# Sums placed beside values, act ends summed on TensorE, two more places for y, and later scaling in a two-act attention kernel

## The reference, cut to what matters

```
x = x + squared(layernorm(x))   # linear-attention layer: scores squared, causal, divided by their sum
x = x + gated(layernorm(x))     # softmax attention, keys and values picked per token by a top-1 gate
x = x + mqa(layernorm(x))       # softmax attention, one key and value head for all query heads
x = x + gated(layernorm(x))
# squared: q, k normalised over the head's 32 channels after gamma and beta
attn = where(causal, einsum(q, k) ** 2, 0);  o = einsum(attn, v) / (sum(attn) + EPS);  o @ Wo.T
# gated, mqa
att = softmax(where(causal, q k / sqrt(32), -inf));  y = einsum(att, v)   # mqa: then y @ out_w.T + out_b
```

## Time and profile before

| | |
|---|---|
| median of 3 runs | 3931.25 us |
| profiled execution | 3928.55 us |
| its span, first to last instruction | 3926.8 us |
| mean granted TensorE clock | 0.982 |
| PE busy | 3609.9 us (92%) |
| POOL busy | 2977.9 us (76%) |
| DVE busy | 2146.6 us (55%) |
| ACT busy | 1621.9 us (41%) |

### The profile page before, as it was taken

How to read it: one execution, slowest core, us unless ns; L and a number is a source line. 1 busy time by engine, 2 the same in 40 slices (tenths; PEclk the granted TensorE clock), 3 DMA queues, 4 the chain that set the end, 5 groups by cost and what they waited for, 6 DMA issues and landing times.

```text
span 3926.8 us, 66685 instructions
## 1 busy us (share of the span) xinstructions
PE 3609.9 (92%) x25570; PEld 1449.9 (37%) x25570; DVE 2146.6 (55%) x5132; ACT 1621.9 (41%) x2433; POOL 2977.9 (76%) x2207
## 2 busy tenths in 40 slices
PE   7999999997999999999888898998999999999976
PEld 5443434332333333333333333333333333333322
DVE  1222322233466766667666666565666666676663
ACT  3554545555033333434444434343333334343333
POOL 4988788897067777778888888887768677686786
PEclk9999999999999999999999999999999999999987
DMA  2001101011110110200101010100101001010010
GB/s 75 28 6 33 33 22 44 9 63 38 49 33 1 31 36 1 65 1 24 43 17 49 7 49 12 36 31 20 47 1 41 25 9 57 1 55 1 7 39 33
DMA packets 63286, 115.02 MB, mean 29 GB/s; under 512 B 8576, under 2 KB 9088, under 8 KB 62976
## 3 DMA queue, kind: packets, MB, share of 16 engines
q1 hardware_dynamic: 62976, 110.75, 8.7%
HBM read 77.17 MB, written 33.55 MB: 28 GB/s over the span
## 4 chain that ended last, share of the span: by engine, by line
PE 60%; ACT 5%; DVE 4%; POOL 3%; issue 2%; DMA 0%; POOLq 0%; ACTq 0%; DVEq 0%
PE banks L1144 12%; PE banks L1191 11%; PE banks L1238 10%; PE banks L1176 9%; PE banks L1137 8%; ACT probs_soft L880 4%; PE banks L1173 4%; PE banks L1337 2%; POOL added_soft L791 2%; DVE banks L976 1%; DVE maxima_soft L971 1%; PE banks L1205 1%; PE banks L1321 1%; POOL added_soft L784 0%; PE banks L1150 0%
## 5 line engine op out<-in xcount | busy, mean ns | idle before, releaser
L880 ACT ACTIVATE probs_soft<-banks 128x1024 f32<-128x1024 f32 (+1 forms) x960 | 848.5, 936 | 1147.8 <-PE banks L1176 1110.2
L791 POOL TENSOR_TENSOR added_soft<-added_soft,probs_soft 128x512 f32<-128x512 f32 (+1 forms) x380 | 1153.4, 3035 | 20.9 <-POOL added_soft L784 5.9
L976 DVE CUSTOM_DVE_ANT_0 banks<-banks,mask 128x128 f32<-128x128 f32 (+3 forms) x1536 | 701.1, 526 | 456.5 <-PE banks L1191 456.2
L971 DVE TENSOR_REDUCE maxima_soft<-banks 128x2 f32<-128x1024 f32 x384 | 452.4, 1221 | 358.7 <-PE banks L1191 358.5
L1191 PE MATMUL banks<-k_soft,q_soft 32*128 32x512 f32 (+3 forms) x4608 | 500.3, 526 | 73.3 <-ACT probs_soft L880 71.7
L1137 PE MATMUL banks<-xnT,wide 128*128 128x512 f32 x1024 | 506.8, 618 | 6.0 <-ACT shift_soft L863 1.9
L886 ACT ACTIVATE probs_squared<-banks,key_scale_squared 128x512 f32<-128x512 f32 (+3 forms) x768 | 379.2, 590 | 316.4 <-PE banks L1176 306.4
L1144 PE MATMUL banks<-wide,xnT 128*128 128x512 f32 x1024 | 498.7, 614 | 0.2 <-ACT shift_soft L863 0.2
L1176 PE MATMUL banks<-q_soft,k_soft 32*128 32x512 f32 (+3 forms) x4608 | 475.1, 495 | 0.0
L784 POOL TENSOR_TENSOR added_soft<-probs_soft 128x2048 f32<-128x2048 f32 x48 | 216.6, 4513 | 329.0 <-ACT probs_soft L880 323.2
L1238 PE MATMUL banks<-probs_soft,v_soft 128*32 128x512 f32 (+3 forms) x4608 | 419.9, 498 | 10.7 <-POOL probs_soft L768 3.8
(11 more groups left out here) (136 smaller groups left out, 4026.2 us busy)
## 6 DMA issues: line engine op xcount, KB each, us to landing
tiles<-out SPq DMA_DIRECT2D x96, 256.0 KB, 2.7
rest_soft<-out SPq DMA_DIRECT2D x96, 256.0 KB, 3.0
out<-rest_soft SPq DMA_DIRECT2D x96, 256.0 KB, 2.1
tiles<-in_x SPq DMA_DIRECT2D x32, 256.0 KB, 2.8
rest_squared<-in_x SPq DMA_DIRECT2D x32, 256.0 KB, 2.8
out<-rest_squared SPq DMA_DIRECT2D x32, 256.0 KB, 2.0
wide<-in_gated_wqkvT SPq DMA_DIRECT2D x3, 1024.0 KB, 7.5
probs_squared<-in_squared_wk SPq DMA_DIRECT2D x1, 1024.0 KB, 5.6
```

What stands on the lines that cost most here:

```text
L791: ins = pool.tensor_tensor(sums, sums, slot(ph, n)[:, :, col:col + width], ALU.add)
L880: ins = act.activation(slot(ph, n)[:, 2 * a:2 * a + 2, 0:width], score_pair(e, a)[:, :, 0:width], ACT.Exp, scale=SCALE)
L971: ins = dve.reduce_max(m["maxima"][:, ph % 2, 2 * a:2 * a + 2, t, p], score_pair(e, a)[:, :, col:col + width], AX_X)
L976: ins = dve.tensor_tensor_reduce(scores, scores, k["mask"][:, CHUNK - width:CHUNK], 1.0, MASKED, ALU.add, ALU.max, m["maxima"][:, ph % 2, ...
```

## The change

`SUMS_AT` puts the sums one half earlier, into the halves that hold values (9 and 15). `LAST_PART` hands bursts 5 and 6 of an act's last phase from POOL's adds to TensorE; the last sum comes ahead of av C and in two steps, all but the last two bursts in the first. The scaling becomes an event behind the first statistics. `y` gets 8 places in act 2. "merged" gets the deadline `2 * HALVES + 4`, and in the last stage of act 2 `3 * HALVES + 4` (it was `2 * HALVES + 6`).

```
-Y_RING = 6
+Y_RING = {False: 6, True: 8}
...
-LAST_PART = (7, 8, 9)
+LAST_PART = (5, 6, 7, 8, 9)
+
+LAST_TWO = (8, 9)
...
-SUMS_AT = (16, 10)
+SUMS_AT = (15, 9)
...
-        events = head[0] + [("raw_weights",), ("own_weights",)] + head[1]
+        events = head[0] + [("raw_weights",), ("own_weights",)] + head[1] + [("scaled",)]
...
-        work += [(parted(merged), 2 * HALVES + 6), (parted(later + first), (3 if kinds[s + 1:s + 2] != ["squared"] else NG) * HALVES - 2),
+        work += [(parted(merged), (3 if soft and s == stages - 1 else 2) * HALVES + 4), (parted(later + first), (3 if kinds[s + 1:s + 2] != ["squared"] else NG) * HALVES - 2),
...
-    events += [("av", last, "C"), ("sm", last, 1), ("last_nrm", last)]
+    events += [("more", ("sm", last, 1)), ("sm", last, 1), ("av", last, "C"), ("last_nrm", last)]
...
-                elif u == "raw_weights":
+                elif u == "scaled":
                     dve.wait_ge(sg.raw_in, DMA * RAW_WEIGHTS)
                     dve.tensor_scalar(m["scaled"][:], k["centre"][:], m["gamma"][:, 0:1], None, ALU.mult).then_inc(sg.scaled, 1)
...
                 elif u == "sm":
                     _, ph, c = e
                     out = free(e)
...
                     final = ph == NG * len(stages) - 1 and c == NC - 1
...
+                    def add_up(cells, q0, width, start, stop):
+
+                        for i in range(HG):
+                            ins = pe.matmul(out[D * i:D * i + D, q0:q0 + width], k["ones"][:], cells[:, i, :], start=start, stop=stop,
+                                            skip_group_check=not soft)
+                        return ins
+
+                    if e not in begun:
+                        if not soft:
+                            pe.wait_ge(sg.query_squares, place["qsq", ph, c] + 1)
+                            pe.matmul(out, k["head_eps"][:].rearrange("p i d -> p (i d)"), m["query_square"][:, c], start=True, stop=True)
+                        pe.wait_ge(sg.probs_added, len(ADDS) * ph + CHUNK_ADDS[c] - (len(LAST_PART) if final else 0))
+                        ins = add_up(m["added"][:, c], 0, CHUNK, soft, not final)
+                        begun[e] = 1
                     if final:
...
+                        for n in LAST_PART[:-len(LAST_TWO)] if opening else LAST_TWO:
+                            pe.wait_ge(sg.probs_ready, 2 * (of_kind["keys", ph, n] + 1))
+                            if KEY_BURSTS[n][1] != "B":
+                                pe.wait_ge(sg.probs_masked, masks_until(ph, None, n))
+                            for kb, q0, width, col in KEY_BURSTS[n][2]:
+                                ins = add_up(slot(ph, n)[:, :, col:col + width], q0, width, False, n == LAST_PART[-1] or not soft)
                     ready(e, ins)
```

More of the change, by code:

```diff
@@ L544, in act_buffers @@
         "q": sb("q", [P, NG, T]),
-        "y": sb("y", [P, Y_RING, T]),
+        "y": sb("y", [P, Y_RING[soft], T]),
         "sums": sb("sums", [P, NC, CHUNK]),
@@ L633, in y_of @@
     def y_of(ph):
-        return m["y"][:, ph % Y_RING, :]
+        return m["y"][:, ph % Y_RING[soft], :]
     def v_of(ph):
@@ L653, in masks_until @@
         masked = [o for o, burst in enumerate(KEY_BURSTS) if burst[1] != "B"]
-        last = n if n is not None else parts_of(part)[0][-1]
+        last = parts_of(part)[0][-1] if n is None else n
         return len(masked) * ph + sum(o <= last for o in masked)
@@ L922, in _ @@
                     c = "AB".index(part)
-                    if ph >= Y_RING and part == "A":
-                        wait_work(act, ("out", (ph - Y_RING) // NG, NT - 1))
+                    if ph >= Y_RING[soft] and part == "A":
+                        wait_work(act, ("out", (ph - Y_RING[soft]) // NG, NT - 1))
                     take_out(e, y_of(ph)[:, CHUNK * c:CHUNK * c + CHUNK], work[:, bank(e), :])
@@ L1198, in _ @@
                     out = free(e)
-                    if not soft:
-                        pe.wait_ge(sg.query_squares, place["qsq", ph, c] + 1)
-                        pe.matmul(out, k["head_eps"][:].rearrange("p i d -> p (i d)"), m["query_square"][:, c], start=True, stop=True)
                     final = ph == NG * len(stages) - 1 and c == NC - 1
[L1203 to L1206, removed]
@@ L1207, in _ @@
-                    if final:
[L1208 to L1213, removed]
+                    def add_up(cells, q0, width, start, stop):
[3 more added lines that the diff above has]
+                        return ins
```

## The result

The kernel after takes 4051.64 us (median of 4 runs, 4044.87 to 4059.35) against 3928.59 of the kernel before (4 runs beside it). The ratio is 1.0309, 95% interval 1.0276 to 1.0341: 3.1% slower, where 0.3% was forecast and the range ended at 3968. Its profiled execution has a span of 4057.6 us and a granted clock of 0.965.

A forecast was written before the change was run, and what follows sets the result against it. TensorE was taken to bound the middle of act 2, POOL's adds the very end. On 3928.55 us: -7.7 - 2.4 - 9 - 1.5 + 34 = +13.4, so 3942 us; 8-in-10 range 3897 to 3968.

The forecast's parts named there:

- Sums beside values: 128 sums moved directly behind av A or av B, in both acts: +34 us, bounds -27 and +100.
- The length of a wait: A sum behind values waits 0.78 us until ACT empties the bank; 0.65 net of the 0.13 saved.
- count: Sums that find a unit open when values end, and so wait for the bank: 81 of 128.
- The cover: Halves without values lose two covers per phase: 8 bare steps at 1.0 us each, +8.
- The relief: Pieces close waits where sums stood alone in about 48 halves, -14; DVE's row maxima get through sooner, -7.
- The sign that was to confirm the forecast: In TensorE's waits, a new row of sums waiting for ACT's copy of y, some 60 times at 0.7 to 0.8.
- The third rival: Where pieces are scarce, above all mqa stages, 35 halves stand bare instead of 8: 3975 us; chance 0.12.
- Its own sign: The wait of L1191 (rows bursts) for ACT grows beyond 80 us.
- Last but one results: Four transposing units leave phase 45 for 46 and 47, where they hide: gain 1.5 us, bounds -4 to +3 in time.
- Later scaling: At the start, scaling behind the statistics lets the fold start at 15.1 instead of 22.89: gain 7.7 us.
- the end of act 2: Without POOL's adds, 7.6 of TensorE's 7.90 us wait go, and the first reciprocal comes sooner: gain 9, bounds 3 and 11.
- The end of act 1: Chunk 0's product comes 1.6 us sooner and the first reciprocal 0.8: gain 2.4, bounds 0 and 4.

The follow-up runs named there:

- The doubled copy: Kernel after, but ACT copies the values of A and B to y twice and only the second copy frees the bank: 4079.87 us, ratio 1.0375.
- units were closed: Planner ends every open unit before av A and av B: on the kernel after 4085.82 us; with SUMS_AT = (16, 10) there, 3983.86 us.
- the sums alone: Kernel before with SUMS_AT = (15, 9) and nothing else of the change: 4033.51 us, ratio 1.026.
- the filled version with the sums back: Kernel after with SUMS_AT = (16, 10), act 1's old deadline, and four unused matmuls in each of 40 bare steps: 3894.89 us, ratio 0.991.
- sums back: Kernel after with SUMS_AT = (16, 10), so all of the change but the sums beside values: 3931.5 us, ratio 0.9998.
- the same version without fillers: Kernel after with SUMS_AT = (16, 10) and act 1's merged deadline back at 2 * HALVES + 6: 3912.92 us, ratio 0.9957.
- the version with both deadlines back: Kernel after, sums beside values, with merged's deadline back at 2 * HALVES + 6 in both acts: 4033.92 us, ratio 1.0261.

## Why the prediction was wrong

**Sums beside values** is the step that failed: forecast +34, measured alone +102, just above its upper bound of +100. Inside it:

- *The length of a wait* was right, 0.75 measured for 0.78. Its *count* was not: 59 for 81. "Units of four pieces stay open about as often" was the error. With the sum in their half, the values' halves take other pieces, and the order of the kernel after has an open unit at the end of av A in 23 phases of act 2 (38 before). What a wait costs in all stays between two estimates: 0.6 to 0.8 of its length by the doubled copy, 26 to 34 us for the 44 us of them; or 0.9 each, 54 us, if the 59 bare steps that took their place when units were closed cost 1.5 each as the other 34 did.
- *The cover* was mis-sized: "I take 8 of them" bare steps, and there are 32 more (29 in act 2; the sums alone add 31). A stage that is short of pieces gets five (the last gated stage ahead of mqa and the first three mqa stages), the last stage of all six. 1.0 us each was about right for idle time. What was missing was the slow matmuls behind it: 1.5 a step where only bare steps were added. At that price 31 steps are 47 us where 8 stood in the sum, and 55 of the 102 are left for the waits and all else; an estimate, which the split by stages above bears out in its order of size.
- *The relief* (-7 for DVE, -14 for closed waits) never came: those waits grew, to 70.6 and 27.5 us in the rows above.

So of the 68 us by which the term was too small, by these estimates some 39 are the cover and 21 the relief. The errors in the waits work against each other: they are fewer than forecast, and at the dearer estimate each costs more than its net price of 0.65. That their total comes near the forecast is luck.

The sign that was to confirm the forecast appeared, some 60 waits of 0.7 to 0.8, and the time was still far off: it could tell about the waits only. The third rival, the cover gone, named the mechanism and nearly the number, 35 bare steps for 8, but priced it at 27 us, without the clock. Its own sign was a wait of L1191 beyond 80 us. In the stretch of the earlier trace rows that wait grew from 56.7 to 70.6, over the whole run from 71.7 to 90.3; like for like it stayed short of the sign.

Slow matmuls are not all of the lost cover. With every bare step filled, the kernel after runs at 0.986 and is still 111 us above the filled version with the sums back (4005.45 and 3894.89), of which act 1's deadline is 8 to 19: a step filled with unused work takes that work's time, 1.16 us, where a sum had stood that has to be made anyway.

The trace of before had the clue. The earlier trace rows show phase 46 at a clock of 0.73 with TensorE busy 43.64 of 60 us. I read this as room in which pieces hide; it was the price of bare steps, already being paid: 11 of the 40 stand in this phase. The whole phase before, and with these steps filled (sums back):

```profile
3799.10:3861.30 62.20, 44.98 (x364) 15.86 (x368) 32.05 (x84) 20.97 (x27) 42.48 (x32) 0.73 0.00 1
```

```profile
3784.80:3834.80 50.00, 44.52 (x449) 22.96 (x448) 31.91 (x84) 20.97 (x27) 42.22 (x32) 1.00 0.00 1
```

Against the same version without fillers, this phase gives 11.2 of the 16.6 us between the two profiled executions.

**Last but one results**: forecast -1.5, bounds -4 to +3. Its premise failed, that four units leave phase 45 for 46 and 47. In the written-out order of neither kernel does one of them stand behind phase 45. With the sums back the deadline moves nothing in act 2; beside values it moves one unit from phase 44 to 45 and costs 9.6. And the diff's `+ 4` also holds in act 1, which the forecast passed over: 16 to 19 us with the sums back, 8 to 12 beside values.

**Later scaling** (-7.7) and **the end of act 2** (-9) were right: 7.4 and 9.7 in the trace with the sums back. **The end of act 1** was forecast at -2.4. The waits went, but from phase 15 to act 2's first matmul it was 89.7 for 90.0: at a clock of 0.84 instead of 0.88 TensorE was busy 4.7 us longer. The three together were forecast at -19.1 and measured at -14 to -17.

**What stays open.** With sums beside values, the start and the ends should make the version with both deadlines back some 15 us faster than the sums alone (start 7.4, act 1's end 2.4, act 2's end 5.2, by the starts of the phases in the two traces). Their profiled executions differ by 13, their medians not at all (4033.92 and 4033.51); with spreads of 4 and 16 us that isn't settled. Nor is the share of the waits in the 102 us, between 26 and 54. And in two places, phase 14 of act 1 and phases 45 and 46 of act 2, the move of a piece or two changed the clock by more than any count of bare steps explains.

## What to carry to other kernels

Moving a short unit to a better place also takes it away from the place where it stood: count the steps that are left with nothing in them, in the written-out order, before pricing the move. The same order shows whether a changed deadline moves anything at all: here one that was priced, and run on its own, moved nothing. Where TensorE is nearly full, price such a step with the slower matmuls behind it, and read a stretch with low granted clock in the profile as a loss to be filled rather than as room. If nothing useful can be put there, unused matmuls can pay: here 80 matmuls of 128 columns, two in each of 40 steps, took 0.5% off (ratio 0.9957 to 0.9905).

## What was not expected of the hardware

Short waits stood right ahead of a fall of TensorE's clock from 2.4 to 1.2 GHz: behind waits of 1.30 and 1.40 us in act 2's phase 23 the same 8 matmuls took 1.89 us for 1.02. The second fall in that phase stands behind waits of 1.29 and 1.58. The 59 single waits of 0.75 us for a bank did not do this: lengthened to 1.37 us they left the mean clock at 0.969 (0.965), and with all bare steps filled it was 0.986 with them and 0.985 without. And two matmuls of 128 columns in a step kept it as high as four did: 0.991 and 0.992. Nor is the clock the same in every execution of one order: phase 45 of act 2 took 55.7 us at a clock of 0.89 in the trace of the sums alone and 51.9 at 0.98 in that of the kernel after with both deadlines back, with the same instructions.
